# Expert up-projection: a signal after each half, and a wait of its own for each bank

## The reference

```python
x = x + xcond(layernorm(x), cond, ctx)      # attention 1 and 2, gated feed-forward
h = layernorm(x)
# a small router gives each token its two best experts and their weights
for e in range(8):                           # F = 352
    a, g = split(h @ w1[e].T, 2)             # up-projection, 128 -> 2 x 352
    out += where(expert == e, (silu(a) * g) @ w2[e].T, 0)
x = x + sum over the two experts of out * weight
```

## Time and profile before

| | us |
|---|---|
| median of 3 runs (lowest, highest) | 2146.03 (2144.26, 2146.51) |
| the profiled execution | 2165.7 |
| its span, first to last instruction | 2163.8 |
| busy: TensorE, weight loads | 2056.7, 1349.0 |
| busy: ScalarE, VectorE, GpSimd | 1403.1, 1328.3, 1065.3 |
| TensorE's mean granted clock | 0.988 |

### The profile page before, as it was taken

The page is one execution under the profiler, slowest core; times in us unless marked ns, Lnnn a source line. Parts: engine busy times, 40 slices in busy tenths (PEclk is TensorE's granted clock), DMA queues, the critical chain, the costliest instruction groups (busy, mean ns, idle before and its releaser), DMA issues. The chain is left out here.

```text
span 2163.8 us, 38718 instructions
## 1 busy us (share of the span) xinstructions
PE 2056.7 (95%) x11132; PEld 1349.0 (62%) x11132; DVE 1328.3 (61%) x3405; ACT 1403.1 (65%) x2665; POOL 1065.3 (49%) x1198
## 2 busy tenths in 40 slices
PE   6899999999999999999999999999999897798996
PEld 5455556555556656555555565656565576788995
DVE  4554657676767666666666676666657654455565
ACT  4566666666767676767676767676766656565663
POOL 1443444636363737373737373736454263555653
PEclk9999999999999999999999999999999999999998
DMA  4111111111111111111211112121113121112266
GB/s 131 46 33 34 49 35 50 45 49 44 53 44 48 44 48 46 50 57 38 58 39 53 52 41 53 39 53 44 44 50 110 45 57 48 51 53 68 61 187 204
DMA packets 136322, 127.36 MB, mean 59 GB/s; under 512 B 14665, under 2 KB 110569, under 8 KB 136234
## 3 DMA queue, kind: packets, MB, share of 16 engines
q1 hardware_dynamic: 127466, 109.11, 18.1%
q0 software_dynamic: 8768, 17.20, 2.4%
HBM read 86.63 MB, written 40.67 MB: 59 GB/s over the span
## 5 line engine op out<-in xcount | busy, mean ns | idle before, releaser
L1860 POOL TENSOR_TENSOR pr<-pr,sm 128x512 f32<-128x512 f32 x256 | 277.4, 1097 | 492.4 <-DVE sm L1414 492.4
L1090 ACT ACTIVATE kp<-ps 128x512 f32<-128x512 f32 x512 | 298.4, 600 | 182.4 <-PE ps L281 178.1
L816 PE MATMUL ps<-tt,V 128*128 128x512 f32 x768 | 381.2, 594 | 3.5 <-ACT tt L1090 3.5
L1404 DVE TENSOR_REDUCE mx<-ps 128x8 f32<-128x512 f32 x256 | 176.8, 691 | 312.8 <-PE ps L765 312.8
L1090 ACT ACTIVATE tt<-ps 128x512 f32<-128x512 f32 x512 | 274.9, 590 | 40.3 <-PE ps L795 40.2
L765 PE MATMUL ps<-kp,hf 128*64 128x256 f32 x2048 | 277.0, 392 | 7.2 <-DVE pr L1407 3.8
L281 PE MATMUL ps<-cT,M 128*128 128x512 f32 x768 | 260.5, 462 | 0.0
L765 PEld LDWEIGHTS ps<-kp,hf 128*64 128x64 f32 x2048 | 124.4, 136 | 197.7 <-DVE pr L1407 139.2
L281 PE MATMUL ps<-hk,M 128*128 128x512 f32 x768 | 244.5, 441 | 1.9 <-DVE hk L1468 1.9
L1090 ACT ACTIVATE pt<-ps 128x512 f32<-128x512 f32 x256 | 153.4, 599 | 141.9 <-PE ps L777 139.4
L917 PE MATMUL ps<-xT,wt 128*128 128x128 f32 (+1 forms) x1728 | 224.5, 281 | 17.2 <-DVE ux L1674 7.6
(11 more groups left out here) (228 smaller groups left out, 3584.7 us busy)
## 6 DMA issues: line engine op xcount, KB each, us to landing
mod<-emb_s SPq DMA_DIRECT2D x96, 256.0 KB, 4.3
xr<-rows_s SPq DMA_DIRECT2D x144, 66.0 KB
cb<-y_s SPq DMA_DIRECT2D x32, 256.0 KB, 5.3
x_in<-in_x_dram SPq DMA_DIRECT2D x16, 256.0 KB, 4.4
xn_s<-x_in SPq DMA_DIRECT2D x16, 256.0 KB, 2.0
res<-xn_s SPq DMA_DIRECT2D x16, 256.0 KB, 2.7
c_in<-in_ctx_dram SPq DMA_DIRECT2D x16, 256.0 KB, 4.8
y_s<-res SPq DMA_DIRECT2D x16, 256.0 KB, 2.0
```

The source lines that it names most:

```text
L816: mm = nc.tensor.matmul(psO[:], Vw[a][:, g * HG + head_at(h), :], tt[:, h, :], start=(g == 0 and h == 0), stop=ends)
L1090: return nc.scalar.activation(o, i, ACT.Copy)
L1404: nc.vector.tensor_reduce(mx[:, p % 2, :], heads(psS[p % 2][:]), AX_X, ALU.max).then_inc(max_done, 1)
L1860: tensor(v, v, sm[:, p, :].unsqueeze(2).broadcast_to([P, HG, 64]), ALU.mult).then_inc(prob_done, 1)
```

## The change

The up-projection is split into two calls of a new function `half_up`, one for each bank. Each half raises `up_pe` by one at its last matmul, so a tile raises it twice, and all who wait for it count in halves. The first half waits for ScalarE's copies and, for the bank, for silu of the tile that used it before. The second half waits for VectorE's copy of the weights and for the gate product of that tile. Silu waits for the first half alone; the gate product now waits for silu and for the second half. `copy_a(n)` waits only for the first half of n-2.

```diff
--- before.py
+++ after.py
@@ -902,19 +902,24 @@
                 nc.tensor.transpose(bX[:, 0:P], xr[:, r, 0:D], ident[:]).then_inc(xt_pe, 1)
 
             def up(n, r):
-                pe.wait_ge(wa_cp, n + 1)
-                pe.wait_ge(wg_cp, n + 1)
-                pe.wait_ge(xt_cp, n + 1)
+                b = pair(n) if isinstance(n, int) else r % 2
                 used = pair_user(n) if isinstance(n, int) else n - 2
                 if isinstance(n, int) and n < EARLY_TILES and pair(n) == 1 and places[n] > glu_to and places[used] < glu_from:
                     pe.wait_ge(glu, FT * NC)
-                if not isinstance(n, int) or used is not None:
+                pe.wait_ge(wa_cp, n + 1)
+                pe.wait_ge(xt_cp, n + 1)
+                if used is not None:
                     pe.wait_ge(sil_done, used + 1)
+                half_up(bA[b], r, 0)
+                pe.wait_ge(wg_cp, n + 1)
+                if used is not None:
                     pe.wait_ge(u_done2, used + 1)
-                b = pair(n) if isinstance(n, int) else r % 2
-                for bank, at in ((bA[b], 0), (bG[b], F)):
-                    for k, w in FK:
-                        mm = nc.tensor.matmul(bank[0:w, k * P:(k + 1) * P], wt[:, r % 2, at + k * P:at + k * P + w], xT[:, r % 2, :], start=True, stop=True)
+                half_up(bG[b], r, F)
+
+            def half_up(bank, r, at):
+
+                for k, w in FK:
+                    mm = nc.tensor.matmul(bank[0:w, k * P:(k + 1) * P], wt[:, r % 2, at + k * P:at + k * P + w], xT[:, r % 2, :], start=True, stop=True)
                 mm.then_inc(up_pe, 1)
 
             def down(n, r):
@@ -1238,7 +1243,7 @@
             def copy_x(n, r):
                 act.wait_ge(xt_pe, n + 1)
                 if not (isinstance(n, int) and n < 2):
-                    act.wait_ge(up_pe, n - 1)
+                    act.wait_ge(up_pe, 2 * n - 2)
                 copy(xT[:, r % 2, :], bX[:, 0:P]).then_inc(xt_cp, 1)
 
             places_now = [act.alloc_register(f"a{next(serial)}") for r in range(TB)]
@@ -1253,11 +1258,11 @@
             def copy_a(n, r):
 
                 if not (isinstance(n, int) and n < 2):
-                    act.wait_ge(up_pe, n - 1)
+                    act.wait_ge(up_pe, 2 * n - 3)
                 copy(wt[:, r % 2, 0:F], WEf[:, bass.ds(place_of(r), F)]).then_inc(wa_cp, 1)
 
             def silu(n, r):
-                act.wait_ge(up_pe, n + 1)
+                act.wait_ge(up_pe, 2 * n + 1)
                 if not (isinstance(n, int) and n < 2):
                     act.wait_ge(u_done2, n - 1)
                 nc.scalar.activation(sl[:, r % 2, :], bA[pair(n) if isinstance(n, int) else r % 2][:, 0:3 * P], ACT.Silu).then_inc(sil_done, 1)
@@ -1669,6 +1674,7 @@
 
             def gate_mul(n, r):
                 dve.wait_ge(sil_done, n + 1)
+                dve.wait_ge(up_pe, 2 * n + 2)
                 if not (isinstance(n, int) and n < 2):
                     dve.wait_ge(y_pe, n - 1)
                 tensor(ux[:, r % 2, :], bG[pair(n) if isinstance(n, int) else r % 2][:, 0:3 * P], sl[:, r % 2, :], ALU.mult).then_inc(u_done2, 1)
@@ -1685,7 +1691,7 @@
             def copy_g(n, r):
 
                 if not (isinstance(n, int) and n < 2):
-                    dve.wait_ge(up_pe, n - 1)
+                    dve.wait_ge(up_pe, 2 * n - 2)
                 nc.vector.tensor_copy(wt[:, r % 2, F:2 * F], WEf[:, bass.ds(place_of(r) + F, F)]).then_inc(wg_cp, 1)
 
             def copy_d(n, r):
```

## The result

The changed kernel takes 2138.83 us (2138.18 to 2141.65, 7 runs) where the kernel before takes 2145.09 (2143.25 to 2146.51, 7 runs): ratio 0.9974, 95% interval 0.9965 to 0.9983, so 6.3 us by the medians. Predicted were 2135.4, with 2126.5 to 2144.5 as the range. Sign and range hold; the gain is three fifths of what was forecast.

A forecast was written before the change was run, and what follows sets the result against it. Only TensorE's idle time in some 390 us of expert tiles could be gained. Terms 5.0 + 1.8 + 4.6 + 2.0 + 0.5 - 1.0 = 12.9 us, discounted to 10.7, gave 2135.4 us, range 2126.5 to 2144.5.

The forecast's parts named there:

- Nothing in steady tiles: Undisturbed tiles, 2.11 us each: TensorE has no idle time there, so earlier silu and product gain nothing.
- Shared pair of banks: Tiles 12 to 28: the first half of the up-projection runs in eight gaps ahead of its loads, 5.0 us.
- feed-forward behind the product: Feed-forward work queued on VectorE behind the gate product comes earlier with silu in four places, 1.8 us.
- the discount: Three quarters kept of shared banks, feed-forward and single late copies (8.8), for gains lost to the next wait: 12.9 becomes 10.7.
- VectorE's late copy, bursts: Last stretch, four bursts of three tiles: the first half no longer waits for VectorE's weight copy, 4 x 0.66 = 2.6 us.
- Single late copies: Some eight late VectorE weight copies before the bursts, of 0.15 to 0.66 us each, 2.0 us together.
- Late signals: Nine tiles between 1955 and 2050 us where silu is released late: down-projection earlier by 0.52 each if signals escape, 2.0 us taken.
- escapes or doesn't: In late-signal tiles: the first half's signal escapes the hold and silu runs inside it, or it is held and nothing changes.
- Last tile: Last down-projection waits 0.71 us for the gate product; earlier silu takes 0.5 of that.
- Added cost: Register operations for doubled counts in rolled loops, about three a tile on ScalarE and two on VectorE: 1.0 us lost.
- Code loading: Rival: longer rolled loops fetch code again, 18 holds, 17 us lost against 10.6 won, 2152 us; chance 0.07.
- I scale nothing: Gain priced on the 2165.7 us profile was taken unscaled, but for rounding, off the 2146.0 us median, 0.9% less.

The follow-up runs named there:

- e12: The kernel before, unaltered, profiled once more on a slower chip: one execution, 2162.1 us.
- e2: The changed kernel, unaltered, timed and profiled again on a slower chip: 2153.2 us against 2164.8 for the kernel before, ratio 0.9947.
- e4: Changed kernel with the separate wait for each bank, but silu still waits for the whole up-projection: 2160.0 us against 2164.8 for the kernel before, ratio 0.9975.
- e3: Changed kernel with silu after the first half, but TensorE waits for everything ahead of that half: 2164.1 us against 2164.8 for the kernel before, ratio 0.9989.
- e6: Kernel before plus second signal and doubled counts only; all waits in front, silu behind both halves: 2168.3 us against 2164.6, ratio 1.0014.
- e10: Changed kernel with GpSimd's eight extra row scatters issued two tiles later: 2148.2 us against 2161.7 for the kernel before, ratio 0.9938.
- e5: The changed kernel, unaltered, run once more on another slower chip: 2157.0 us against 2164.6 for the kernel before, ratio 0.9967.

## Why the prediction was right or wrong, step by step

*Nothing in steady tiles*: right. Silu is 0.54 us earlier and the tile stays at 2.11. Whoever books 0.5 us in 144 tiles is off by 66 us.

*Shared pair of banks, 5.0, and feed-forward behind the product, 1.8, of both three quarters (5.1)*: the window gains 4.0 us on the slower chips (65.2 to 61.2; the list of gaps takes 0.69 three times where its rule says 0.66, which is 0.1 of the 5.0). The mechanism of the first holds: tiles 15 and 19 go from 2.83 to 2.11 in both traces. It is partly given back within the ring, as the discount assumed: tile 20 goes from 4.47 to 5.08. The second step failed. Over the same tiles, e12 and then e2, silu's group and the feed-forward's loads that wait for the gated product:
```profile
L1263 ACT ACTIVATE sl<-ps 128x384 f32<-128x384 f32 x15 | 7.4, 491 | 11.5 <-PE ps L917 8.1 <-remote 2.1 <-issue 1.2
...
L281 PEld LDWEIGHTS ps<-gl,W 128*128 128x128 f32 x9 | 1.5, 188 | 4.3 <-DVE gl L1524 3.1 <-issue 1.1
```
```profile
L1268 ACT ACTIVATE sl<-ps 128x384 f32<-128x384 f32 x15 | 7.3, 490 | 2.4 <-PE ps L922 1.5 <-remote 0.8
...
L281 PEld LDWEIGHTS ps<-gl,W 128*128 128x128 f32 x12 | 1.9, 188 | 4.9 <-DVE gl L1529 3.7 <-issue 1.0
```
The loads stand 4.3 us idle for three groups of three and 4.9 for four: 1.4 and 1.2 us a group, hardly less. Silu waits 9 us less, and 4 us of time come of it, nearly all in the up-projection's own gaps (11.1 to 7.0 in the same two traces).

*VectorE's late copy, bursts, 2.6*: right in place and size on the slower chips (71.6 to 68.8, 2.8), and more where VectorE waits less for the transfers of its chunks (4.7 in e4 and on the faster chip, with waits of 1.7 and 2.9 us against 4.1 and 4.5). e3 against e4 shows that this is the separate wait's work alone. *Single late copies, 2.0*: failed. Tiles 2, 6 and 9 do gain 0.17, 0.51 and 0.44, but tiles 10 to 13 lose as much (tile 11: 4.20 to 4.75), and tiles 0 to 13 together take 39.7 us before and after. In tiles 29 to 63 the kernel before itself varies by 4 us; nothing can be read there.

*Late signals, 2.0*: the mis-sized step. 94.7 to 94.2, 0.5 us. The prediction's alternative was "escapes or doesn't". Both happen: in most late tiles the first signal escapes, and the second one, for which the product waits since this very change, doesn't. And in about half of these tiles the down-projection waits for neither but for its bank, which ScalarE empties on a signal that is held as well. The gain that this leaves went to the later scatter; with a semaphore for each half it is 3.0 to 3.7. On the faster chip, where the kernel was timed, there was probably nothing to gain: the changed kernel has no late tile there, and the kernel before is faster there by as much (19.5 us against 18.2), though no trace of it was taken.

*Last tile, 0.5*: failed, 0. From its up-projection to its end it takes 3.73 us in every trace. The prediction overlooked the wait for the down-projection's bank, here as in the late tiles.

*Added cost, 1.0*: neither confirmed nor refuted. e6 shows 3.0 (1.1 to 5.0), but 0.6 of it is the order of the waits and 1.2 lies where the counts are constants; the remaining 1.2 would fit the forecast. It is not in the steady tiles, which stay at 2.11. About two instructions a tile were added on ScalarE (135 in the profile, over 72 tiles) and one on VectorE (47, over the 40 tiles of its rolled part), where the prediction had three and two.

*Code loading*: didn't come, no hold at any seam; on the faster chip every tile from 62 to 109 takes 2.11.

The sum of what is measured on the slower chips, -4.0 - 2.8 - 0.5, with 0.5 in tiles 104 to 112 and 1.3 in tiles 29 to 63 (inside that stretch's variation), is the 9.1 of the lengths. Forecast were 10.7. That this is near is in part luck: of the 9.1, 7.3 stand on terms of the forecast, and late signals, single copies and last tile gave 0.5 where 4.0 were booked after the discount. What was missed is that the trace belonged to another chip than the median that it was set against: "I scale nothing" passed over the one sign of it, 0.9% between profile and runs.

## What to carry to other kernels

Before a trace's waits are priced, set its execution time against the timed runs; if they differ, ask which waits would vanish at the shorter time, and price the change without these. A signal that is split helps only as far as its last consumer: follow each of the new waits to the instruction behind it, and list every count that this instruction waits for, not the one that the view names. In a rolled loop a semaphore for each half adds fewer instructions than doubled counts, and the traces were 1.6 to 3.3 us shorter in tiles 64 to 103, though the times can't tell. Look for work that is bunched on the engine that sets the pace: spreading VectorE's additions took 5.7 us off these tiles, where the change took 9.1.

## What the hardware showed unexpectedly

Beside an indirect row scatter on GpSimd, TensorE's signals to the other engines can be held back until some 3.1 us after its start (in some tiles 2.3 or 1.6), on some chips. It moved with the scatter in e10. GpSimd's 144 ordinary scatters do no such thing in most tiles. What sets the eight and the late tile 101 apart is that scatters are bunched there. The rows of the kernel before at tile 100, with silu of that tile:
```profile
2041.67 0.99 POOL L1970 DMA_INDIRECT y_s<-yo,tg  x1 [3.08 <-issue]
...
2043.05 1.00 POOL L1970 DMA_INDIRECT y_s<-yo,tg  x1 [0.16 <-issue]
...
2044.44 0.99 POOL L1970 DMA_INDIRECT y_s<-yo,tg  x1 [0.16 <-issue]
2044.51 0.49 ACT L1263 ACTIVATE sl<-ps 128x384 f32<-128x384 f32 x1 [1.51 <-PE ps L917]
```
Three scatters start within 2.77 us, with no extra one among them; beside an extra scatter it is some 2.65 us. In each of the 13 traces from slower chips, among tiles 60 to 143, three start within 3.0 us at nine places, and just these are followed by the late tiles named here. That bunching is the cause is inferred; no run spread the scatters, and on the faster chip they are as close and nothing is held. There the same rows at tile 80 read:
```profile
1979.49 1.39 PEld L922 LDWEIGHTS ps<-xT,wt 128*128 128x128 f32 x12
1980.06 0.96 POOL L1953 DMA_INDIRECT rows_s<-rows,ridx  x1 [0.30 <-issue]
1980.78 0.47 ACT L1268 ACTIVATE sl<-ps 128x384 f32<-128x384 f32 x1
...
1981.29 0.56 DVE L1680 TENSOR_TENSOR ux<-ps,sl 128x384 f32<-128x384 f32 x1 [0.50 <-ACT sl L1268]
```
The product follows the scatter's start by 1.23 us and not 3.0. Between the changed kernel's traces on the faster chip and in e5 the first up-projection starts within 0.1 us (1761.0 and 1760.9), and the tiles take 359.8 and 378.5: the difference between these chips for this kernel, 18.2 us, lies wholly in the tiles, more than half of it (9.8) in tiles 64 to 103.
